# The last batch of a Mamba-and-MoE block in two halves of its tokens

## The chip, the cores and the metric

The kernel runs on one core of one Trainium2 chip. The core has five engines that run side by side and meet through semaphores: PE (TensorE, matmuls and transposes), DVE (VectorE), ACT (ScalarE), POOL (GpSimd) and SP (SyncE, which here issues all DMAs). The metric is the device time of one execution in microseconds, lower is better.

## The reference

The input x is 8 batches of 1024 tokens of 256 channels. One adaptive-norm block is computed, with six modulation vectors per batch from a small matmul:

```
h = layernorm(x) * (1 + ca) + sa
dt, B, C from h (64-wide, 16-wide, 16-wide projections); dt = softplus(...)
state[n] = exp(dt * A[n]) * state[n] + dt * h * B[n]     # 16 states per channel, along the tokens
x = x + ga * (sum over n of state[n] * C[n] + h * D)
h = layernorm(x) * (1 + cb) + sb
x = x + gb * (gated sum of the top 2 of 8 experts, each 256 x 256, with bias)
```

## The kernel before

**Units.** A batch has 256 channels x 16 states = 4096 rows of 1024 tokens. They are worked in 32 units of 128 rows: two halves of the channels (hf), four groups of states (q), four groups of channels (j). For a unit ACT writes the decay into av (`exp`, L544), DVE forms dt·u·B in the PSUM banks BP from B spread over the partitions in the banks BQ and from dd (`mul`, L728), DVE scans along the 1024 tokens into one of 8 buffers h (`scan`, L735), POOL multiplies by C in place (`ch`, L845). After four units PE sums their rows into the PSUM banks Y (`y`, L412) and spreads the next B (`Bs`, L393). After 16 units DVE adds the skip path (`zs`, the skip product, L758), after 32 PE transposes (`z`, L487) and DVE adds the residual (`zX`, L768).

**Before and behind.** Ahead of its units a batch is normalised from XN, transposed, projected, and dt passes softplus in four pieces of 128 channels x 512 tokens (`dl`, five operations on ACT, L578 to L590; `corr` on DVE, L752; `dt`, three on POOL, L854 to L859) in src; SP copies src to dd, four DMAs for each of j and of dt and dt·u (`ddt`, L340; `ddu`, L347). Src holds one hf, so the pieces of the next hf wait for the copies. Behind its units a batch gets statistics (`stat`, L641, L644), `rstd`, `rsb` (L741), normalisation (`xh`, L656), transposes (`xT`), logits (`lg`), their transpose (`lT`), the top 2 (`soft` and `top`, 17 small operations on DVE, L779 to L795), gates through DRAM (`gT`, `gw`, `gr`, `gl`), and the experts: 4 blocks of 256 tokens x 4 pairs of experts. A step takes POOL's product of tokens and gates (`xg`, L877) and 16 matmuls (`f`, L504); a block ends with bias (L509), ACT's read-out (`fE`, L626), transposes (`o`, L476), the add (`oX`, L773) and the store (`out`).

**Order.** Each engine runs its steps in one fixed order. `schedule` gives every step a planned time in units, from the table AT and the batch's start 32·b, sorts them all, and every engine takes its own from the list. So the numbers of AT set the order within an engine and nothing else; the true times come from waits. `before(b)` is placed one batch early, `after(b)` one batch late: the experts of batch 6 stand among the scans of batch 7. The `Bank` class hands out PSUM banks for the small steps; after the last scan the idle banks BP and BQ serve too (TAIL).

## Time and profile before

| | us |
|---|---|
| median of 3 runs | 1278.88 (1278.57 to 1281.31) |
| profiled execution | 1282.32, of which the span is 1280.4 |
| busy: PE, DVE, ACT, POOL | 965.2, 1059.5, 707.2, 1024.5 |
| granted clock of PE, mean | 0.848 of full |

Times of the trace count from the start of the span. A row of a timeline gives start, duration, engine, line, operation, output<-inputs, number of instructions merged, and in brackets the engine's idle time before with what released it.

### The profile page before, as it was taken

The numbers are of one execution on the slowest core, as the hardware profiler recorded it, in microseconds if no ns is written. First come the engines' busy times: TensorE is split into PE (matmuls) and PEld (weight loads), VectorE is DVE, ScalarE is ACT, GpSimd is POOL, SyncE is SP. The second block draws the span as 40 slices with busy tenths as digits, with TensorE's granted clock in tenths as the row PEclk, the third lists the DMA queues.
The fourth block names the chain that finished last, engine by engine and source line by source line (L and its number), as shares of the span: only waits on it lengthen the run. The fifth ranks groups of instructions, "written<-read, shape, count | busy, mean of one in ns | idle before, by whom it ended". The sixth has DMA issues, their size and how long they took to land. (4 is left out here: it accounts for less than half of the span.)

```text
span 1280.4 us, 13483 instructions
## 1 busy us (share of the span) xinstructions
PE 965.2 (75%) x4232; PEld 604.6 (47%) x4232; DVE 1059.5 (83%) x793; ACT 707.2 (55%) x1348; POOL 1024.5 (80%) x512
## 2 busy tenths in 40 slices
PE   5334444588878897788878887789778896789798
PEld 4101112255554564355644655356445564467576
DVE  1399999999999999898999999999989999992100
ACT  5754567555765568465755667456755474333200
POOL 1476777599997999699978999699969999796253
PEclk9665655689888998798988998799879999899799
DMA  4606150636244451537155433436162624412121
GB/s 156 150 15 164 44 121 1 149 105 156 61 111 121 113 143 48 143 100 181 42 118 143 115 105 76 123 108 173 34 157 76 148 75 115 120 47 66 43 75 58
DMA packets 90536, 131.20 MB, mean 102 GB/s; under 512 B 13529, under 2 KB 73505, under 8 KB 90465
## 3 DMA queue, kind: packets, MB, share of 16 engines
q1 hardware_dynamic: 90464, 130.34, 39.2%
q8 instruction: 34, 0.56, 0.2%
q14 instruction: 38, 0.30, 0.1%
HBM read 54.50 MB, written 8.65 MB: 49 GB/s over the span
## 5 line engine op out<-in xcount | busy, mean ns | idle before, releaser
L845 POOL TENSOR_TENSOR h<-h,Cr 128x1024 f32<-128x1024 f32 x256 | 602.0, 2368 | 131.2 <-DVE h L735 131.0
L735 DVE TENSOR_TENSOR_SCAN h<-av,ps 128x1024 f32<-128x1024 f32 x256 | 585.0, 2285 | 18.3 <-DVE ps L728 0.9
L504 PE MATMUL ps<-xg,we 128*128 128x256 f32 x2048 | 514.7, 409 | 29.8 <-POOL xg L877 22.4
L504 PEld LDWEIGHTS ps<-xg,we 128*128 128x128 f32 x2048 | 412.2, 206 | 137.4 <-issue 44.8
L544 ACT ACTIVATE av<-dd,An 128x1024 f32<-128x1024 f32 x256 | 289.9, 1142 | 141.5 <-DVE h L735 134.2
L877 POOL TENSOR_TENSOR xg<-h2T,gbc 128x1024 f32<-128x1024 f32 x128 | 303.5, 2372 | 76.5 <-DMA gbc<-gates 35.3
L728 DVE TENSOR_TENSOR ps<-ps,dd 128x1024 f32<-128x1024 f32 x256 | 315.4, 1232 | 39.9 <-DMA dd<-src 14.1
L412 PE MATMUL ps<-h,gam 128*32 128x512 f32 x1024 | 165.1, 775 | 32.3 <-POOL h L845 17.6
L393 PE MATMUL ps<-S,sel 64*128 64x512 f32 x128 | 56.0, 523 | 65.0 <-DVE ps L728 64.1
L773 DVE TENSOR_TENSOR X<-ps,X 128x512 f32<-128x512 f32 x32 | 22.0, 688 | 99.3 <-PE ps L476 99.1
L598 ACT ACTIVATE Cr<-ps 128x512 f32<-128x512 f32 x64 | 37.9, 593 | 94.5 <-PE ps L453 63.2
L626 ACT ACTIVATE z<-ps,md 128x256 f32<-128x256 f32 x64 | 26.6, 466 | 104.5 <-PE ps L509 104.5
L412 PEld LDWEIGHTS ps<-h,gam 128*32 128x32 f32 x1024 | 31.7, 128 | 109.6 <-issue 84.0
L393 PEld LDWEIGHTS ps<-S,sel 64*128 64x128 f32 x128 | 22.9, 222 | 106.8 <-DVE ps L728 93.8
L854 POOL TENSOR_TENSOR src<-src,sp_t 128x512 f32<-128x512 f32 x32 | 40.7, 1273 | 30.9 <-DVE sp_t L752 30.9
L453 PE MATMUL ps<-S,sel 64*128 64x512 f32 x64 | 34.4, 541 | 40.2 <-ACT Cr L598 26.8
L446 PE MATMUL ps<-rows,wrow 64*128 64x512 f32 x64 | 44.1, 775 | 11.2 <-DVE S L746 8.0
L560 ACT ACTIVATE hT<-ps,md 128x512 f32<-128x512 f32 x32 | 24.5, 770 | 50.7 <-PE ps L432 50.7
L432 PE MATMUL ps<-identf,sp_t 128*128 128x128 f32 x128 | 22.1, 302 | 37.8 <-ACT sp_t L656 31.1
L453 PEld LDWEIGHTS ps<-S,sel 64*128 64x128 f32 x64 | 13.1, 206 | 66.9 <-ACT Cr L598 35.9
L432 PE MATMUL ps<-identf,XN 128*128 128x128 f32 x128 | 26.4, 344 | 22.4 <-DVE S L746 10.1
L859 POOL TENSOR_TENSOR src<-src,hT 128x512 f32<-128x512 f32 x32 | 40.8, 1274 | 2.5
(96 smaller groups left out, 861.8 us busy)
## 6 DMA issues: line engine op xcount, KB each, us to landing
dd<-src SPq DMA_DIRECT2D x512, 128.0 KB, 2.4
gbc<-gates SPq DMA_DIRECT2D x128, 256.0 KB, 3.5
X<-in_x SPq DMA_DIRECT2D x8, 1024.0 KB, 7.3
...
```

Source lines behind the costliest of these rows:

```text
L393: e = pe.matmul(ps[:, BQ + c], sel[R:P, q], S[R:P, b % 2, c * CH:(c + 1) * CH], start=True, stop=True)
L412: e = pe.matmul(ps[32 * j:32 * j + 32, Y + c], gam[:, b % 2, 2 * j + hf], h[:, (4 * g + j) % HS, c * CH:(c + 1) * CH], start=(q == 0), sto ...
L432: e = pe.transpose(bk[:, q * P:(q + 1) * P], (XM[:, q] if w else XN[:, 4 * c + q])[:, hf * P:(hf + 1) * P], identf[:])
L446: e = pe.matmul(bk, wdt[:, hf * P:(hf + 1) * P], dtr[:, c * CH:(c + 1) * CH], start=True, stop=True)
L453: e = pe.matmul(bk, sel[R:P, NQ + q], S[R:P, b % 2, c * CH:(c + 1) * CH], start=True, stop=True)
L504: e = pe.matmul(ps[:, FB, m * 256:(m + 1) * 256], we[:, hf, 2 * ep + e2, m * P:(m + 1) * P], xg[:, i % XG, e2, hf], start=(ep == e2 == m = ...
L544: act.activation(av[:, u % AS], dd[:, j, 0], ACT.Exp, scale=An[:, 0, i:i + 1]).then_inc(s_a, 1)
L728: dve.tensor_tensor(wide(BP), wide(BQ), dd[:, j, 1], ALU.mult).then_inc(s_bm, 1)
L735: dve.tensor_tensor_scan(h[:, u % HS], av[:, u % AS], wide(BP), 0.0, ALU.mult, ALU.add).then_inc(s_scan, 1)
L845: pool.tensor_tensor(h[:, u % HS], h[:, u % HS], Cr[:, q], ALU.mult).then_inc(s_ch, 1)
L859: pool.tensor_tensor(src[:, 1, cs], src[:, 0, cs], hT[:, b % 2, hf, cs], ALU.mult).then_inc(s_dtu, 1)
L877: pool.tensor_tensor(xg[:, i % XG], h2T[:, :, 256 * c:256 * c + 256].unsqueeze(1).to_broadcast([P, 2, 2, 256]), gbc[:, i % GL].unsqueeze(2 ...
```

## The change

Batch 7 (LAST) is worked in 64 half units: 32 over tokens 0 to 511, then 32 over tokens 512 to 1023. `ring` gives each half unit half a buffer of h and av, so there are 16 and 6 places. ACT copies the last column of each state of the first half into `kept` (`keep`), and the scan of the second half starts from it; POOL's product, which overwrites that column, waits for the copy. The banks of b (BP) and B (BQ) alternate, one of each per half unit and per spread. The loads of dd come in four sets of 512 columns (128 DMAs in place of 64), the softplus pieces in the order of the token halves. `zs`, `z`, `zX`, statistics, norm, routing, gates and experts run per half, with planned times of their own (names ending in A and B). The tail banks serve the second half only. In the planner the half units stand 0.55 apart from 3.59 behind the batch's start (`late`), and all other constants of AT have new values as well, so the order of the other batches can shift too. The routing's small tensors, the gates' DMAs and the semaphores are split in the same way (not shown).

```diff
 P, BLK, CH = 128, 8, 512
 NQ, NJ = 4, 4
 UB = 2 * NQ * NJ
-TOTAL = NB * UB
+LAST = NB - 1
+SPLIT = UB * LAST
+TOTAL = SPLIT + 2 * UB
 HS, AS, XG, GL = 8, 3, 2, 2
 EPS = 1e-5
+PACE = 0.55
 BP, BQ, Y, FB, MB = 0, 2, 4, 6, 7
-AT = dict(exp=-1.21, mul=1.08, scan=1.53, ch=6.84, Bs=0.19, y=7.26, stat0=-5.28, stat0s=0.98, rstd0=3.61,
-          rsb0=1.59, xh0=11.0, xh0s=0.0, xT0=14.39, xT0h=1.94, xTs=3.73, rxT0=-0.6, wx=5.18, rwx=-0.33, S=0.3,
-          ldx=33.57, gam=38.49, dl0=20.77, dl1=35.27, dls=3.25, rdl=-0.37, corr=1.62, dt=7.73, C=25.76,
-          CS=2.56, Cc=2.97, rC=-0.32, ddt=36.17, ddts=1.47, ddu=36.38, ddus=1.74, zs=4.09, ldx2=32.55, z=3.84,
-          zX=1.16, zd=1.62, stat1=4.55, stat1s=0.63, rstd1=9.44, rsb1=0.73, xh1=9.97, xh1s=0.0, xh1g=1.34,
-          xT1=11.24, xT1h=0.62, xT1s=1.34, rxT1=-0.73, lg=13.33, rlg=0.11, lT=0.58, rlT=-0.25, soft=2.26,
-          softe=-1.82, top=2.7, gT=1.83, rgT=-0.99, gw=11.19, gr=34.34, xg=22.19, xgs=1.74, gl=-2.54, f=-2.35,
-          fE=0.24, o=2.15, oX=3.12, out=15.62, md1=-34.13, gates=-49.65, ga=-3.38)
+AT = dict(exp=-0.77, mul=1.64, scan=2.24, ch=6.45, Bs=-0.01, y=6.85, stat0=-5.1, stat0s=0.67, rstd0=1.17,
+          rsb0=3.44, xh0=3.56, xh0s=0.32, xT0=13.59, xT0h=2.02, xTs=3.63, rxT0=0.32, wx=4.29, rwx=0.92,
+          S=1.74, ldx=31.71, gam=35.11, dl0=19.88, dl1=34.98, dls=3.7, rdl=0.32, corr=2.11, dt=5.91, C=25.77,
+          CS=3.43, Cc=0.88, rC=0.44, ddt=40.03, ddts=0.91, ddu=41.44, ddus=1.19, zs=4.96, ldx2=33.63, z=4.89,
+          zX=1.12, zd=1.59, stat1=5.89, stat1s=0.4, rstd1=8.89, rsb1=2.35, xh1=9.83, xh1s=0.14, xh1g=1.0,
+          xT1=10.69, xT1h=0.46, xT1s=1.53, rxT1=0.06, lg=12.73, rlg=0.79, lT=0.36, rlT=0.75, soft=3.62,
+          softe=-2.05, top=3.65, gT=1.45, rgT=0.36, gw=14.19, gr=35.16, xg=21.62, xgs=1.76, gl=-5.61, f=-2.15,
+          fE=0.55, o=2.87, oX=4.07, out=18.16, md1=-39.19, gates=-31.77, ga=-39.94, dtL=6.8, dlL0=19.7,
+          dlL1=28.05, dlL2=35.27, dlL3=38.79, defer=-0.1, ddL=-4.28, late=3.59, expL=-3.77, mulL=0.2,
+          scanL=0.49, chL=13.21, BsL=-3.79, yL=10.36, zsL=9.04, keep=1.26, zA=4.6, zB=14.77, zXA=1.0,
+          zXB=19.05, zdA=39.81, zdB=5.99, stat1A=5.26, stat1B=18.11, stat1sA=0.0, stat1sB=0.0, rstd1A=5.8,
+          rstd1B=23.04, rsb1A=1.57, rsb1B=23.92, xh1A=6.93, xh1B=29.62, xh1sA=0.0, xh1sB=1.09, xh1gA=5.05,
+          xh1gB=69.25, xT1A=8.3, xT1B=35.72, xT1hA=1.57, xT1hB=12.51, xT1sA=40.02, xT1sB=22.36, rxT1A=0.0,
+          rxT1B=15.64, lgA=10.75, lgB=60.74, rlgA=0.68, rlgB=7.79, lTA=1.53, lTB=10.67, rlTA=1.33, rlTB=0.15,
+          softA=2.56, softB=43.82, softeA=1.66, softeB=-25.94, topA=3.13, topB=44.68, gTA=7.7, gTB=32.21,
+          rgTA=1.12, rgTB=14.09, gwA=23.22, gwB=64.93, grA=49.62, grB=127.0, xgA=32.58, xgB=140.39,
+          xgsA=12.14, xgsB=14.47, glA=-3.23, glB=14.59, fA=8.35, fB=5.67, fEA=6.12, fEB=12.1, oA=1.07,
+          oB=64.82, oXA=54.06, oXB=87.4, outA=41.88, outB=47.69)
...
-            put(s + AT["corr"], "corr", b, hf, c)
-            put(s + AT["dt"], "dt", b, hf, c)
-        s = t + 16 * hf
+    for i in range(4):
+        hf, c = (i % 2, i // 2) if b == LAST else (i // 2, i % 2)
+        s = t + (AT["dl1" if hf else "dl0"] + AT["dls"] * c if b < LAST else AT[f"dlL{i}"])
+        put(s, "dl", b, hf, c)
+        put(s + AT["rdl"], "read", "dl", b, hf, c)
+        put(s + AT["corr"], "corr", b, hf, c)
+        put(s + AT["dtL" if b == LAST and i > 1 else "dt"], "dt", b, hf, c)
+    for i in range(4 if b == LAST else 2):
+        s = t + (PACE * 16 * i + AT["ddL"] * min(i, 1) if b == LAST else 16 * i)
         for j in range(NJ):
-            put(s + AT["ddt"] + AT["ddts"] * j, "ddt", 2 * b + hf, j)
-            put(s + AT["ddu"] + AT["ddus"] * j, "ddu", 2 * b + hf, j)
+            put(s + AT["ddt"] + AT["ddts"] * j, "ddt", 2 * b + i, j)
+            put(s + AT["ddu"] + AT["ddus"] * j, "ddu", 2 * b + i, j)
     for q in range(NQ):
         for c in range(2):
             s = t + AT["C"] + AT["CS"] * q + AT["Cc"] * c
...
-    for i in range(UB):
-        for n in ("exp", "mul", "scan", "ch"):
-            put(t + i + AT[n], n, UB * b + i)
-    for i in range(2 * NQ):
-        put(t + 4 * i + AT["Bs"], "Bs", 2 * NQ * b + i)
-        put(t + 4 * i + AT["y"], "y", 2 * NQ * b + i)
-    for hf in range(2):
-        put(t + 16 * hf + 16 + AT["zs"], "zs", b, hf)
+    n, pace, own = UB, 1, ""
+    if b == LAST:
+        n, pace, t, own = 2 * UB, PACE, t + AT["late"], "L"
+    for i in range(n):
+        for name in ("exp", "mul", "scan", "ch"):
+            put(t + pace * (i + AT[name + own]), name, UB * b + i)
+        if i < n - UB:
+            put(t + pace * (i + AT["keep"]), "keep", UB * b + i)
+    for i in range(n // 4):
+        put(t + pace * (4 * i + AT["Bs" + own]), "Bs", 2 * NQ * b + i)
+        put(t + pace * (4 * i + AT["y" + own]), "y", 2 * NQ * b + i)
...
-def after(b, t, put):
-    for kp in range(2):
-        s = t + AT["z"] + AT["zd"] * kp
+def after(b, t, put, part=None):
+    halves = range(2) if part is None else (part,)
+    times = AT if part is None else {n: AT[n + "AB"[part]] for n in HALF}
+    blocks = [k for c in halves for k in range(4 * c, 4 * c + 4)]
+    tag = (b,) if part is None else (b, part)
+    for i, kp in enumerate(halves):
+        s = t + times["z"] + times["zd"] * i
         put(s, "z", b, kp)
-        put(s + AT["zX"], "zX", b, kp)
-    for k in range(BLK):
...
         beside(b, UB * b, put)
-        after(b, UB * (b + 1), put)
+        if b < LAST:
+            after(b, UB * (b + 1), put)
+    for part in range(2):
+        after(LAST, SPLIT + AT["late"] + PACE * UB * (part + 1), put, part)
     return [step for _, step in sorted(at, key=lambda p: p[0])]
...
 def unit(u):
-    b, r = divmod(u, UB)
-    return b, r // 16, r // 4 % 4, r % 4
+    b, c = (u // UB, None) if u < SPLIT else (LAST, (u - SPLIT) // UB)
+    return b, u // 16 % 2, u // 4 % 4, u % 4, c
+def piece(b, hf, c):
+    return 4 * b + (2 * c + hf if b == LAST else 2 * hf + c)
+def loads(H):
+    if H < 2 * LAST:
+        return 2 * H + 1, H - 1, 0, 64 * (H + 1)
+    i = H - 2 * LAST
+    return 4 * LAST + i, 2 * LAST - 1 if i < 2 else H - 2, i % 2, 64 * (i // 2 + 1 + (2 * LAST if i % 2 == 0 else 0))
+def ring(u, n):
+    if u < SPLIT:
+        return u % n, slice(0, L), u - n
+    m = SPLIT + (u - SPLIT) // 2
+    return m % n, slice(u % 2 * CH, u % 2 * CH + CH), m - n if m - n < SPLIT else u - 2 * n
+def place(H):
+    return slice(0, L) if H < 2 * LAST else slice(H % 2 * CH, H % 2 * CH + CH)
...
             return self.HEAD
-        if s[:3] == ("xT", 1, NB - 1) or s[0] in ("lg", "lT", "gT", "o") and s[1] == NB - 1:
+        if s[:4] == ("xT", 1, LAST, 1) or s[0] in ("lg", "lT", "gT") and s[1:] == (LAST, 1):
+            return self.TAIL
+        if s[0] == "o" and s[1] == LAST and s[2] >= 2:
             return self.TAIL
...
+                    last, old, r, _ = loads(H)
+                    sp.wait_ge(s_dt, last + 1)
                     if H:
-                        sp.wait_ge(s_a, 16 * (H - 1) + 12 + j + 1)
+                        sp.wait_ge(s_a, 16 * old + 12 + j + 1)
                     for nl in range(4):
-                        sp.dma_start(dd[32 * nl:32 * nl + 32, j, 0], src[32 * j:32 * j + 32, 0]).then_inc(s_ddt[j], 16)
+                        sp.dma_start(dd[32 * nl:32 * nl + 32, j, 0, place(H)], src[32 * j:32 * j + 32, 0, place(H)]
+                                     ).then_inc(s_ddt[r][j], 16)
...
                     for c in range(2):
                         emptied(pe, ("wx", b, c))
-                if g:
-                    pe.wait_ge(s_bm, 4 * g)
-                for c in range(2):
-                    e = pe.matmul(ps[:, BQ + c], sel[R:P, q],
-                                  S[R:P, b % 2, c * CH:(c + 1) * CH], start=True, stop=True)
+                if half is None:
+                    if g:
+                        pe.wait_ge(s_bm, 4 * g)
+                    for c in range(2):
+                        e = pe.matmul(ps[:, BQ + c], sel[R:P, q], S[R:P, b % 2, c * CH:(c + 1) * CH], start=True, stop=True)
...
+                elif q == 0:
+                    pe.wait_ge(s_zr, 2 * b + half)
+                    pe.wait_ge(s_z, 2 * b + 2 * half)
...
+                n, cols, old = ring(u, AS)
+                if old >= 0:
+                    act.wait_ge(s_scan, old + 1)
                 i = 16 * hf + 4 * j + q
-                act.activation(av[:, u % AS], dd[:, j, 0], ACT.Exp, scale=An[:, 0, i:i + 1]).then_inc(s_a, 1)
+                act.activation(av[:, n, cols], dd[:, j, 0, place(u // 16)], ACT.Exp,
+                               scale=An[:, 0, i:i + 1]).then_inc(s_a, 1)
...
-                        for j in range(NJ):
-                            act.wait_ge(s_ddt[j], 64 * (2 * b + hf))
-                            act.wait_ge(s_ddu[j], 64 * (2 * b + hf))
+                    if b == LAST and i % 4 >= 2:
+                        copied(act, 2 * LAST + i % 4 - 2)
+                    elif i % 2 == 0 and i:
+                        copied(act, i // 2 - 1)
...
+                elif s[0] == "keep":
+                    u = s[1]
+                    act.wait_ge(s_scan, u + 1)
+                    n, cols, _ = ring(u, HS)
+                    act.activation(kept[:, u - SPLIT:u - SPLIT + 1], h[:, n, cols.stop - 1:cols.stop], ACT.Copy).then_inc(s_keep, 1)
...
+                if half is None:
+                    dve.tensor_tensor(wide(BP), wide(BQ), dd[:, j, 1], ALU.mult).then_inc(s_bm, 1)
+                else:
+                    dve.tensor_tensor(ps[:, BP + u % 2], ps[:, BQ + u // 4 % 2], dd[:, j, 1, place(u // 16)], ALU.mult).then_inc(s_bm, 1)
...
             def scan(u):
-                if u >= HS:
-                    dve.wait_ge(s_y, (u - HS) // 4 + 1)
+                half = unit(u)[-1]
+                n, cols, old = ring(u, HS)
+                if old >= 0:
+                    dve.wait_ge(s_y, old // 4 + 1)
                 dve.wait_ge(s_bm, u + 1)
                 dve.wait_ge(s_a, u + 1)
-                dve.tensor_tensor_scan(h[:, u % HS], av[:, u % AS], wide(BP), 0.0, ALU.mult, ALU.add).then_inc(s_scan, 1)
+                hu, a = h[:, n, cols], av[:, ring(u, AS)[0], cols]
+                if half is None:
+                    dve.tensor_tensor_scan(hu, a, wide(BP), 0.0, ALU.mult, ALU.add).then_inc(s_scan, 1)
+                else:
+                    i = (u - SPLIT) % UB
+                    start = 0.0
+                    if half:
+                        dve.wait_ge(s_keep, i + 1)
+                        start = kept[:, i:i + 1]
+                    dve.tensor_tensor_scan(hu, a, ps[:, BP + u % 2], start, ALU.mult, ALU.add).then_inc(s_scan, 1)
             def beside_scan(s):
                 if s[0] == "rsb":
...
+                    hf, z, y = i, hT[:, b % 2, i % 2], wide(Y)
+                    if b == LAST:
+                        hf = i % 2
+                        z, y = z[:, i // 2 * CH:(i // 2 + 1) * CH], ps[:, Y + hf]
+                    dve.scalar_tensor_tensor(out=z, in0=z, scalar=Dga[:, hf, b:b + 1], in1=y, op0=ALU.mult,
...
+                n, cols, _ = ring(u, HS)
+                hu, cq = h[:, n, cols], Cr[:, q]
+                if half is not None:
+                    cq = cq[:, half * CH:(half + 1) * CH]
+                    if half == 0:
+                        pool.wait_ge(s_keep, u - SPLIT + 1)
+                pool.tensor_tensor(hu, hu, cq, ALU.mult).then_inc(s_ch, 1)
```

## Rows read from the trace of the kernel before

**Rows 1.** The page's costliest groups: three of them, busy us, mean ns | idle before, releaser.

```profile
L845 POOL TENSOR_TENSOR h<-h,Cr 128x1024 f32<-128x1024 f32 x256 | 602.0, 2368 | 131.2 <-DVE h L735 131.0
L735 DVE TENSOR_TENSOR_SCAN h<-av,ps 128x1024 f32<-128x1024 f32 x256 | 585.0, 2285 | 18.3 <-DVE ps L728 0.9
...
L877 POOL TENSOR_TENSOR xg<-h2T,gbc 128x1024 f32<-128x1024 f32 x128 | 303.5, 2372 | 76.5 <-DMA gbc<-gates 35.3
```

**Rows 2.** Busy time of each engine in four stretches, times from the span's start.

```profile
739.20:876.80 137.60, 112.95 (x518) 71.82 (x517) 131.86 (x96) 84.93 (x162) 123.89 (x60) 0.90 0.43 111
1018.50:1154.30 135.80, 107.43 (x503) 70.87 (x502) 127.27 (x93) 61.28 (x103) 124.74 (x58) 0.90 0.37 95
1154.30:1205.80 51.50, 39.53 (x208) 30.81 (x207) 10.86 (x24) 18.90 (x54) 21.19 (x10) 0.89 0.16 48
1205.80:1280.40 74.60, 67.16 (x288) 55.83 (x288) 2.77 (x4) 3.36 (x8) 35.17 (x15) 0.91 0.23 68
```

**Rows 3.** Timeline of DVE in batch 7: start us, us, line, operation [idle before].

```profile
1019.97 1.23 DVE L728 TENSOR_TENSOR ps<-ps,dd 128x1024 f32<-128x1024 f32 x1 [1.46 <-PE ps L393]
...
1082.42 0.19 DVE L779 TENSOR_REDUCE gs<-ga_t 128x8 f32<-128x64 f32 x1
...
1131.98 1.23 DVE L728 TENSOR_TENSOR ps<-ps,dd 128x1024 f32<-128x1024 f32 x1
1133.30 2.29 DVE L735 TENSOR_TENSOR_SCAN h<-av,ps 128x1024 f32<-128x1024 f32 x1
1135.63 1.23 DVE L728 TENSOR_TENSOR ps<-ps,dd 128x1024 f32<-128x1024 f32 x1
```

**Rows 4.** Four lines by themselves: duration in ns, min/median/max, first and last start.

```profile
L773 DVE TENSOR_TENSOR X<-ps,X x32: 680/691/693, 294.7 to 1277.1; 128x512 f32<-128x512 f32 x32
...
L758 DVE SCALAR_TENSOR_TENSOR hT<-hT,Dga,ps x16: 1270/1276/1281, 129.1 to 1158.8; 128x1024 f32<-128x1024 f32 x16
...
L741 DVE TENSOR_TENSOR rs<-rs x16: 159/1080/3905, 22.5 to 1180.0; 128x8 f32<-128x8 f32 x16
...
L859 POOL TENSOR_TENSOR src<-src,hT x32: 1261/1274/1285, 40.0 to 1063.4; 128x512 f32<-128x512 f32 x32
```

**Rows 5.** Timeline of POOL, batch 7 and the end.

```profile
1021.27 4.67 POOL L845 TENSOR_TENSOR h<-h,Cr 128x1024 f32<-128x1024 f32 x2
...
1092.83 2.36 POOL L845 TENSOR_TENSOR h<-h,Cr 128x1024 f32<-128x1024 f32 x1 [7.31 <-DVE h L735]
1097.67 2.35 POOL L877 TENSOR_TENSOR xg<-h2T,gbc 128x1024 f32<-128x1024 f32 x1 [2.48 <-DMA gbc<-gates]
...
1154.37 2.35 POOL L845 TENSOR_TENSOR h<-h,Cr 128x1024 f32<-128x1024 f32 x1 [0.32 <-DVE h L735]
...
1203.39 4.65 POOL L877 TENSOR_TENSOR xg<-h2T,gbc 128x1024 f32<-128x1024 f32 x2 [18.06 <-DMA gbc<-gates]
```

**Rows 6.** Timeline of PE, the last sums of batch 6.

```profile
1029.86 1.92 PE L412 MATMUL ps<-h,gam 128*32 128x512 f32 x16
```

**Rows 7.** Timeline of ACT, the first exponential behind the third piece's softplus.

```profile
1035.84 1.15 ACT L544 ACTIVATE av<-dd,An 128x1024 f32<-128x1024 f32 x1
```

**Rows 8.** Timeline of SP's queue, four loads of dd.

```profile
1023.50 2.50 SPq L347 DMA_DIRECT2D dd<-src  x4
```

**Rows 9.** Timeline of PE, first steps of the last two expert groups.

```profile
1243.15 3.69 PE L504 MATMUL ps<-xg,we 128*128 128x256 f32 x16 [1.02 <-ACT z L626]
...
1259.72 3.69 PE L504 MATMUL ps<-xg,we 128*128 128x256 f32 x16 [1.02 <-ACT z L626]
```

**Rows 10.** Timeline of ACT, first statistic of two blocks in a row.

```profile
1164.99 0.42 ACT L641 ACTIVATE junk<-X 128x256 bf16<-128x256 f32 x1 [12.82 <-DVE X L768]
...
1166.17 0.42 ACT L641 ACTIVATE junk<-X 128x256 bf16<-128x256 f32 x1
```

**Rows 11.** Timeline of DVE, first and last of 17 routing operations, batch 7.

```profile
1192.71 0.22 DVE L779 TENSOR_REDUCE gs<-ga_t 128x8 f32<-128x64 f32 x1 [11.26 <-ACT ga_t L605]
...
1196.73 0.22 DVE L795 TENSOR_TENSOR ga_t<-ga_t,gs 128x64 f32<-128x64 f32 x1
```

281 lines of the change are left out of this document (165 added, 116 removed).

## The prediction

> **What bounds the kernel now.** I read the groups of instructions first, then the stages, then the order of time around the last batch. The costliest groups are POOL's product by C and DVE's scan, 256 of each; DVE idled 18.3 us before all its scans together [rows 1]. The reader is to see two engines close to full. In a middle period of 137.6 us DVE is busy 131.9 and POOL 123.9 us. In the last batch's scans (1018.5 to 1154.3) both fall a little, and in the last 126 us DVE does nearly nothing: routing until 1205.8, then 74.6 us with PE alone busy [rows 2]. Seven expert steps of batch 6 are still left at 1156.7. So the end is: scans, a chain of norm and routing that nothing covers, then 16 expert steps on PE. The change shortens this tail and lengthens the scans before it.
>
> The profiled execution took 1282.32 us, 1.9 over its span of 1280.4; the median is 1278.88. I make the sum in span and take the difference from the median.
>
> **Price of a half unit.** A unit (product by dt·u, then scan) repeats every 3.65 us, 1.32 to the scan and 2.33 to the next product [rows 3]. A product of 512 columns from PSUM takes 0.691 [rows 4], against 1.23 for 1024 [rows 3]: 0.15 of it is fixed. A scan of 2.29 with the same fixed part gives 1.22 (bounds: 1.14, half, and 1.45). With the gaps seen (0.08 and 0.03) a half unit is 2.03 us, two of them 4.06: +0.41 for each of 32 pairs, 13 us on DVE. POOL: 1.274 for 512 columns [rows 4] against 2.36, a full one repeating every 2.33 (two in 4.67 [rows 5]), so a half one every 1.25: 64 of them 80 us, +5.5.
>
> **The kept states.** 32 copies of one column on ACT lie between its exponentials; for 32 pairs of halves ACT has some 2.0 us per DVE half unit and needs 0.7 (an estimate from the 1.15 of 1024 columns [rows 7]) plus 0.2. I cost them at nothing; where ACT is stuck in another wait, POOL's product waits behind it (rival 2). The scan of a second half reads its start value from SBUF beside av. Such a scalar stands in the skip product, whose 16 runs lie between 1270 and 1281 ns whatever POOL does, while small operations with two SBUF tensors stretch from 159 to 3905 ns [rows 4]. I take +0.04 each, 1.3 us (bounds 0 and, as if stopped, a whole POOL half, 1.25 x 32 = 40).
> The Trainium skill, SBUF — State Buffer, section "SBUF: two separate sides", says that DVE and GpSimd share a port pair as an exclusive lock, which a DVE operation with two SBUF inputs takes against GpSimd. If the kept column counted as such an input, 32 scans would each wait half a POOL product on average, some 20 us; by the skip product's row it doesn't count.
>
> **Up to the routing of batch 6.** Before, DVE goes from 1019.97 to the routing at 1082.42: 62.45 us, 15 units (54.7) and 7.8 of other work [rows 3]. In the new order the routing (16.25 behind the batch's start) stands behind scan 22, since scan u stands at 3.86 + 0.55u. So 23 half units, 46.7, and 7.8: 1074.5 if nothing stalls. I add three stalls. (1) The skip product of batch 6 stands behind 3 half units instead of behind 3 units and a product. It needs POOL's last two products of batch 6, which start at 1021.27 [rows 5], and their sums, which end at 1031.8 [rows 6]; DVE is there at 1026.8: 5 us. (2) ACT's softplus of the second pair of pieces stands behind exponential 3 and lets ACT back at 1035.8 [rows 7]; now it has half units to cover it: 1 us. (3) The fourth piece overwrites source columns that the loads of the new second quarter must have left. Each set of four loads holds SP for 2.5 us [rows 8], eight sets 20 us, behind the first quarter's: until some 1046, while ACT, with the kept copies and exponentials from the 11th on, stands behind it; DVE's correction of that piece stands behind scan 9, due about 1048 with the piece at 1050: 2 us (bounds 0, if an issue of 64 KB is cheaper, and 8). Sum 8: routing at 1082.5, where it was. The first half's dd loads for the second token half have 16 half units of lead and are hidden.
>
> **From the routing to the last product by C.** From routing to the first expert product it is 15.25 us, 1082.42 to 1097.67 [rows 3, 5], the same operations: 1097.8. POOL's order then decides. The product of unit u stands at 10.86 + 0.55u, the expert product k of batch 6 at 21.52 + 1.76k: 20 half products stand before the first expert product, and 14 expert products before the last half product (45.5). Before it was 16 and 9. POOL then has 44 x 1.25 + 14 x 2.33 = 87.6 us without a gap: last product done at 1185.4, against 1156.7 (1154.37 + 2.35 [rows 5]): +28.7. DVE isn't the bound here: from 1089 it has 41 half units (83), two skip products, one residual add, one rsb, the routing of half A (4.3, with POOL in its way 6) and three adds, about 97 us: 1186 if nothing overlaps worse, so the two engines are near each other, and I take POOL's. The double banks of B take away waits such as the 1.46 us before 1019.97 [rows 3]; these are off the bound then.
>
> **The tail.** PE's order is written: sums, expert steps 14 and 15 of batch 6, transposes of half B, then half A's 8 steps with B's transposes, logits and gates between steps 1 and 6, then half B's 8. From the last product on: sums 1.1 and 1.3 for the expert product; two steps of 3.5 with bias and read-out 2.2, out-transposes 0.6 and residual transposes 1.0: 13.2. Half A, two groups at the period of 16.57 (1243.15 to 1259.72 [rows 9]): 33.1. B's pieces on PE between them 2.6. Stalls: B's statistics are 4 blocks of 1.18 [rows 10], with rstd, rsb and four normalisations 8.5 us behind the residual add, beside two steps of 3.5: 2.7. Its 17 small operations take 4.2 (1192.71 to 1196.95 [rows 11]) beside steps 4 and 5: 0. Step 7's gates stand on SP behind an output of half A whose add stands behind B's routing: 1.5. First B step at +53. From a group's start with two groups left it is 37.25 (1243.15 to 1280.4 [rows 9]). Tail 90.3, against 123.7: -33.4. The B gates leave SP at about +42 and need 5.7 (POOL from 1203.39 [rows 5]): hidden under steps 6 and 7, with 3 us to spare.
>
> Sum: +28.7 - 33.4 = -4.7: span 1275.7, median 1274.2. The other seven batches keep the order of DVE's operations but for shifts under a unit (rsb and the XN normalisation come earlier), at 0; bounds -1 and +1 us a batch.
>
> **Rivals.**
> 1. The head stalls don't come (POOL and PE finish batch 6 earlier under half units, or SP issues 64 KB faster): routing at 1074.5, C's last at 1177.4, median 1266. For it: SP's durations in rows 8 say nothing of 64 KB. Against: the sums end at 1031.8 whatever DVE does.
> 2. Slower: ACT stands in the fourth piece's wait for the second quarter's loads, and the kept copies from the 6th or so on stand behind it, so POOL stands too, though its columns are scanned. 64 more loads cost 38 us of SP in the batch. If they land 12 us later than the 1046 above, routing comes at 1094.5 and the median is 1286. It decides from 7 us on (then the gain of 4.7 turns into a loss above 0.2%). Before, ACT waited there only for loads of the half before.
> 3. The kept column takes the port (above): 20 us on DVE's second half, which has little slack, +15: 1289. The rows speak against it.
> 4. No change: half A's steps fill PE anyway, and what the halves save is what they cost: within 2.6 us. It is the forecast with 3 us more, in the tail or on POOL.
>
> **How the numbers follow.** The measurement tells 0.2%, 2.6 us, from no change. Forecast 50% (own range 1267 to 1280; of it 36 faster, 12 same, 2 slower); rival 1 22%; rival 2 20%; rival 3 3%; the reordered other batches by themselves 5% (2 faster, 1 same, 2 slower; rival 4 is in the forecast's range). Faster 60%, same 13%, slower 27%. Range 1258 to 1290: rival 1 with the batches' gain below, rivals 2 and 3 above.
>
> **What would show it.** Scans of 1.22 and products by C of 1.27; no idle POOL between its first batch-6 expert product and its last product by C; routing of batch 6 within 3 us of 1082; DVE idle some 5 us before batch 6's last skip product; last product by C at 1180 to 1190; 90 us from there to the end; PE without a gap over 3 us after the first A step. It is wrong if DVE or ACT bounds the second half, if the second half's scans are longer than the first's, or if A's expert steps run among the scans.

## The result and the profile after

The changed kernel takes 1301.41 us, the median of 4 runs (1300.04 to 1302.13), beside 1279.85 for the kernel before on the same chip: ratio 1.0167, 95% interval 1.0149 to 1.0184. Forecast were 1274.2, in a range of 1258 to 1290. It is slower by 21.6 us, and the time lies outside the range. The profiled execution took 1302.13 us with a span of 1300.3, 19.9 more than the span before.

The groups of the page, as in [rows 1], show the operations at the prices that were worked out: the units of the first seven batches are unchanged, and the half units of the last take 1.22 and 1.28 us to scan and 1.25 for the product by C (80.0 us for 64). These are the groups with shapes kept apart:

```profile
L1009 POOL TENSOR_TENSOR h<-h,Cr 128x1024 f32<-128x1024 f32 x224 | 527.4, 2371 | 128.7 <-DVE h L882 127.3 <-ACT Cr L718 1.3
...
L1009 POOL TENSOR_TENSOR h<-h,Cr 128x512 f32<-128x512 f32 x64 | 80.0, 1288 | 12.5 <-DVE h L889 7.1 <-ACT kept L798 5.4
...
L889 DVE TENSOR_TENSOR_SCAN h<-av,kept,ps 128x512 f32<-128x512 f32 x32 | 41.0, 1280 | 2.7
...
L889 DVE TENSOR_TENSOR_SCAN h<-av,ps 128x512 f32<-128x512 f32 x32 | 39.0, 1219 | 3.2 <-DVE ps L871 0.4 <-ACT av L655 0.4
```

So the loss isn't in the price of a half unit. The next view is the busy time in four stretches: a middle batch (from its first scan to the next batch's, the same events as the first row of [rows 2]); from the last scan of batch 6 to 1156.7, inside POOL's mix of products by C and expert products; from there to the end of the last product by C; and the tail. The columns are the stretch, its length, busy PE, PEld, DVE, ACT and POOL with counts, granted clock, DMA share, GB/s:

```profile
749.30:888.20 138.90, 113.41 (x517) 70.31 (x516) 131.53 (x98) 87.07 (x168) 124.40 (x61) 0.90 0.44 113
1031.30:1156.70 125.40, 102.65 (x454) 67.54 (x458) 110.91 (x130) 71.88 (x179) 103.67 (x69) 0.85 0.40 107
1156.70:1201.30 44.60, 35.29 (x173) 23.87 (x166) 41.45 (x50) 9.63 (x19) 37.50 (x27) 0.89 0.19 42
1201.30:1300.30 99.00, 85.41 (x373) 69.00 (x371) 12.93 (x25) 13.84 (x38) 42.28 (x19) 0.91 0.20 59
```

The last scan of batch 6 ends at 1031.3, where before it ended at 1018.5 [rows 2]. The reader is to see that 12.8 of the 19.9 us are there before the first half unit has run, in batches that the halving doesn't touch. The whole decomposition, cut at the same events before and after, in us of span:

| stretch | before | after | change | forecast |
|---|---|---|---|---|
| start to last scan of batch 6 | 1018.5 | 1031.3 | +12.8 | 0 |
| to the first expert product of batch 6 on POOL | 79.2 | 73.5 | -5.7 | 0 |
| to the end of the last product by C | 59.0 | 96.5 | +37.5 | +28.7 |
| to the end of the span | 123.7 | 99.0 | -24.7 | -33.4 |

**Where the first 12.8 us go.** The small product `rsb` (eight columns, two SBUF inputs; L741 before, L896 now) has a line of its own in [rows 4]: 159/1080/3905 ns before. The same view of it after, with the scans beside it:

```profile
L896 DVE TENSOR_TENSOR rs<-rs x17: 141/1904/6792, 22.8 to 1222.7; 128x8 f32<-128x8 f32 x15, 128x4 f32<-128x4 f32 x2
...
L889 DVE TENSOR_TENSOR_SCAN h<-av,kept,ps x32: 1280/1280/1283, 1118.9 to 1198.7; 128x512 f32<-128x512 f32 x32
...
L916 DVE SCALAR_TENSOR_TENSOR hT<-hT,Dga,ps x18: 722/1266/1273, 129.5 to 1204.5; 128x1024 f32<-128x1024 f32 x14, 128x512 f32<-128x512 f32 x4
```

The median is 1.9 us and the longest 6.8, for an operation that takes 0.14 when alone. The scans with a kept start, and the skip product, don't stretch at all. What a long one waits for shows when the timelines of DVE and POOL are laid side by side. DVE in batch 2:

```profile
323.77 2.28 DVE L882 TENSOR_TENSOR_SCAN h<-av,ps 128x1024 f32<-128x1024 f32 x1
325.96 6.49 DVE L896 TENSOR_TENSOR rs<-rs 128x8 f32<-128x8 f32 x1
332.38 1.22 DVE L869 TENSOR_TENSOR ps<-ps,dd 128x1024 f32<-128x1024 f32 x1
```

And POOL at the same time, where a row without brackets follows the one before it without a gap:

```profile
323.06 2.45 POOL L1009 TENSOR_TENSOR h<-h,Cr 128x1024 f32<-128x1024 f32 x1
325.37 2.47 POOL L1042 TENSOR_TENSOR xg<-h2T,gbc 128x1024 f32<-128x1024 f32 x1
327.68 4.75 POOL L1009 TENSOR_TENSOR h<-h,Cr 128x1024 f32<-128x1024 f32 x2
335.45 1.26 POOL L1019 TENSOR_TENSOR src<-src,sp_t 128x512 f32<-128x512 f32 x1 [3.02 <-DVE sp_t L907]
```

`rsb` starts at 325.96 while POOL works and ends at 332.45; POOL's last product ends at 332.43. It has sat out not one operation of POOL but the rest of three, until POOL ran out of work. Then POOL waits in its turn, 3.02 us, for what DVE should have made. At 898.23 it is the same: 6.79 us, to 905.02, and POOL's run ends at 904.99 (900.29 + 4.70).

Not every wait is of this kind. In batch 4 `rsb` gets in behind one product by C, and POOL goes on without a gap:

```profile
648.01 1.90 DVE L896 TENSOR_TENSOR rs<-rs 128x8 f32<-128x8 f32 x1
```

```profile
647.55 2.35 POOL L1009 TENSOR_TENSOR h<-h,Cr 128x1024 f32<-128x1024 f32 x1
649.86 2.35 POOL L1042 TENSOR_TENSOR xg<-h2T,gbc 128x1024 f32<-128x1024 f32 x1
```

Of the 17 `rsb` of this kernel 13 are stretched. Each ends within 0.03 us of the end of an operation of POOL: seven at the first one's end with POOL going on, two where POOL's only operation left ends, four behind two or three operations, at the end of POOL's run. What decides between the two kinds no run shows; the four take 22.6 of the 39.6 us.

The Trainium skill, SBUF — State Buffer, section "SBUF: two separate sides", says that the pair of ports is held "for the whole instruction" by whoever starts first, while the other blocks. The trace agrees that the small product blocks, and nine of the 13 waits fit one instruction of the other. The other four don't: 6.49 us is longer than any POOL instruction in these rows (2.47 at most). The measurement decides.

**The last batch.** A wait of the long kind stands here in the routing of the first half. DVE, with the routing of the first half between the scans:

```profile
1171.65 0.70 DVE L871 TENSOR_TENSOR ps<-ps,dd 128x512 f32<-128x512 f32 x1
1172.26 0.17 DVE L937 TENSOR_REDUCE gs<-ga_t 128x4 f32<-128x32 f32 x1
1172.47 7.23 DVE L938 TENSOR_TENSOR ga_t<-ga_t,gs 128x32 f32<-128x32 f32 x1
1179.73 0.18 DVE L939 TENSOR_SCALAR ga_t<-ga_t 128x32 f32<-128x32 f32 x1
1179.95 1.28 DVE L889 TENSOR_TENSOR_SCAN h<-av,kept,ps 128x512 f32<-128x512 f32 x1
```

POOL works until 1179.65 and is then short of scans:

```profile
1178.34 1.31 POOL L1009 TENSOR_TENSOR h<-h,Cr 128x512 f32<-128x512 f32 x1
1181.31 1.27 POOL L1009 TENSOR_TENSOR h<-h,Cr 128x512 f32<-128x512 f32 x1 [1.66 <-DVE h L889]
1186.91 1.27 POOL L1009 TENSOR_TENSOR h<-h,Cr 128x512 f32<-128x512 f32 x1 [4.33 <-DVE h L889]
...
1193.75 1.27 POOL L1009 TENSOR_TENSOR h<-h,Cr 128x512 f32<-128x512 f32 x1 [0.83 <-DVE h L889]
```

**The tail.** SP's queue has two stores standing before gates that the experts wait for:

```profile
1215.17 0.38 SPq L470 DMA_DIRECT2D out<-X  x1
1215.64 0.91 SPq L465 DMA_DIRECT2D gbc<-gates  x1
...
1245.68 0.38 SPq L470 DMA_DIRECT2D out<-X  x1
1246.15 1.30 SPq L465 DMA_DIRECT2D gbc<-gates  x1
```

POOL, which multiplies tokens by these gates, idles beside them (the first gap is put down to PE, the last to come of two; the gates had only just been asked for at 1215.64):

```profile
1220.26 4.66 POOL L1042 TENSOR_TENSOR xg<-h2T,gbc 128x1024 f32<-128x1024 f32 x2 [9.70 <-PE ps L610]
...
1250.57 2.34 POOL L1042 TENSOR_TENSOR xg<-h2T,gbc 128x1024 f32<-128x1024 f32 x1 [5.69 <-DMA gbc<-gates]
```

### The profile page after: what moved, and what is told of

It reads as the page before. It is cut to its first block and busy times, and to the rows that moved or that the text cites. A ratio compares the mean times of both kernels' runs of the same rounds, so it can differ in the third digit from the quotient of the medians.

```text
span 1300.3 us, 13889 instructions
## 1 busy us (share of the span) xinstructions
PE 983.2 (76%) x4235; PEld 612.4 (47%) x4235; DVE 1090.1 (84%) x877; ACT 724.1 (56%) x1418; POOL 1029.8 (79%) x544
## 5 line engine op out<-in xcount | busy, mean ns | idle before, releaser
L1009 POOL TENSOR_TENSOR h<-h,Cr 128x1024 f32<-128x1024 f32 (+1 forms) x288 | 607.4, 2131 | 141.2 <-DVE h L882 127.3
L882 DVE TENSOR_TENSOR_SCAN h<-av,ps 128x1024 f32<-128x1024 f32 x224 | 511.7, 2284 | 14.9 <-DVE ps L869 0.9
L655 ACT ACTIVATE av<-dd,An 128x1024 f32<-128x1024 f32 (+1 forms) x288 | 299.4, 1047 | 149.6 <-DVE h L882 114.1
L869 DVE TENSOR_TENSOR ps<-ps,dd 128x1024 f32<-128x1024 f32 x224 | 276.0, 1232 | 40.8 <-DMA dd<-src 15.5
L517 PE MATMUL ps<-h,gam 128*32 128x512 f32 x1024 | 157.7, 738 | 19.1 <-POOL h L1009 15.9
L491 PEld LDWEIGHTS ps<-S,sel 64*128 64x128 f32 x112 | 21.0, 232 | 114.3 <-DVE ps L869 101.2
L558 PE MATMUL ps<-S,sel 64*128 64x512 f32 x64 | 36.3, 570 | 30.7 <-ACT Cr L718 23.9
L546 PE MATMUL ps<-hT,wx 128*128 128x512 f32 x64 | 43.6, 818 | 18.2 <-DVE sp_t L907 9.2
L698 ACT ACTIVATE sp_t<-ps,bd 128x512 f32<-128x512 f32 x32 | 21.8, 682 | 55.8 <-PE ps L551 55.7
L781 ACT ACTIVATE sp_t<-X,rs 128x256 f32<-128x256 f32 x64 | 34.0, 588 | 26.0 <-DVE rs L896 26.0
L871 DVE TENSOR_TENSOR ps<-ps,dd 128x512 f32<-128x512 f32 x64 | 44.7, 698 | 3.8
```

The lines of the kernel that those rows point to most:

```text
L491: e = pe.matmul(ps[:, BQ + c], sel[R:P, q], S[R:P, b % 2, c * CH:(c + 1) * CH], start=True, stop=True)
L517: e = pe.matmul(ps[32 * j:32 * j + 32, Y + (c if half is None else hf)], gam[:, b % 2, 2 * j + hf], h[:, n, cols.start + c * CH:cols.start ...
L546: e = pe.matmul(bk, wx[:, k], hT[:, b % 2, k, c * CH:(c + 1) * CH], start=(k == 0), stop=(k == 1))
L655: act.activation(av[:, n, cols], dd[:, j, 0, place(u // 16)], ACT.Exp, scale=An[:, 0, i:i + 1]).then_inc(s_a, 1)
L869: dve.tensor_tensor(wide(BP), wide(BQ), dd[:, j, 1], ALU.mult).then_inc(s_bm, 1)
L871: dve.tensor_tensor(ps[:, BP + u % 2], ps[:, BQ + u // 4 % 2], dd[:, j, 1, place(u // 16)], ALU.mult).then_inc(s_bm, 1)
```

## The experiments

The theory after the result has three parts. **Order:** the new constants of AT, not the halves, cost the first 13 us, because `rsb` of the first norm stands at a place where POOL's runs are long, and DVE waits for them. **Stores:** two stores in SP's order hold gates back, 9 us. **Routing:** the first half's routing waits on the path, up to 7 us. The rival to each is that the halves cost by themselves: kept states, more loads, more waits.

Each kernel has its ratio to the kernel before on the same chip, with a 95% interval. Where a kernel is compared with another of the table, it is by these ratios, or by the medians where that is said.

**1. The new order without the halves.** The kernel before with the shared constants of the new AT; all batches whole.

```diff
-AT = dict(exp=-1.21, mul=1.08, scan=1.53, ch=6.84, ... rstd0=3.61, rsb0=1.59, xh0=11.0, ...
+AT = dict(exp=-0.77, mul=1.64, scan=2.24, ch=6.45, ... rstd0=1.17, rsb0=3.44, xh0=3.56, ...
```

> The kernel before, whole batches, with the new values of the planner's constants (order changes, nothing is halved). Theory A, the new order costs the first seven batches 11 to 13 us whatever the last batch does: about 1291. Rival, those 11 us come with the halving (its queue entries, its loads): 1280. With A, the first norm's rsb (the product of negative mean and rstd on DVE) is stretched in this kernel as in the changed one, 6 us in several batches against 3.9 before.

Measured: 1292.23 us, ratio 1.0102 (1.0082 to 1.0122). The first scan of the last batch starts at 1035.6, against 1021.3 before and 1032.2 in the changed kernel. So the order alone costs 13 us; the halves with all that belongs to them cost the rest, 8 to 9. The 16 `rsb` take 39.5 us here.

**2. The old order under the halves.** The changed kernel; the other batches get the old constants, shifted by one amount for each engine (ACT +0.44, DVE +0.56, POOL -0.39, PE -0.41, SP +3.0) so that they meet the last batch. The first scan constants as an example:

```diff
-AT = dict(exp=-0.77, mul=1.64, scan=2.24, ch=6.45, ...
+AT = dict(exp=-0.77, mul=1.64, scan=2.09, ch=6.45, ...
```

> The changed kernel, last batch in halves, with the old order for all other batches (old constants, each engine's shifted by one amount so that they fit the last batch's). Theory A: 1301 less 11 to 13, about 1289; what is left over 1280 is the halving's own, 9 us. Rival, the order of the first seven batches is innocent: 1300.

Measured: 1311.3 us, ratio 1.0253 (1.023 to 1.0275). A miss. `rsb` does get shorter (1200 ns in the mean of 15), but other waits come in: DVE stands 30.7 us for PE's B, and POOL 53.7 us for gates. The last batch's first scan is at 1044.5; the period before it is 154.3 us. Probably the shifted engines no longer fit one another; that wasn't tested, and this kernel tells nothing of the halves.

**3 and 4. `rsb` off DVE, in both kernels.** The eight columns are multiplied on ACT, one small operation each with the factor as its scale, right behind the rsqrt.

```diff
+                    act.wait_ge(s_rd[w], nth(s[1:]))
+                    for k in range(k0, k1):
+                        e = act.activation(rs[:, w, 5, k:k + 1], rs[:, w, 0, k:k + 1], ACT.Identity, scale=rs[:, w, 4, k:k + 1])
+                    e.then_inc(s_rs[w], 1)
...
-                    dve.tensor_tensor(rs[:, w, 5, k0:k1], rs[:, w, 0, k0:k1], rs[:, w, 4, k0:k1], ALU.mult).then_inc(s_rs[w], 1)
```

> The changed kernel with rsb taken from DVE: 8 (or 4) small operations on ACT behind rstd form the same product. Theory B: DVE's operation with two SBUF inputs waits until POOL's run of operations ends, and these waits (rsb busy 39.6 us in 17 operations, 37 of them waiting) stand on the bound: 1301 less 15 to 30, so 1271 to 1286. Rival, POOL is the bound wherever DVE waits for it, so that nothing is won: 1298 to 1302.

> The kernel before with rsb on ACT in the same way. Theory B: its 16 rsb are busy 25.3 us, 22.7 of them waiting: 1280 less 10 to 20, 1260 to 1270. Rival, POOL is the bound while DVE waits: 1278 to 1281.

Measured: with halves 1266.8 us, ratio 0.99 (0.9884 to 0.9915); the kernel before with the same edit 1266.9, ratio 0.9899 (0.9874 to 0.9923). The edit is worth 34.6 us by the medians in the changed kernel, more than the 15 to 30 expected, and 13 in the one before; the two are then equal. So of the 25.3 us that `rsb` took before, at the prices of [rows 4], about half was on the path all along. The edit also spares ACT the way over DVE and back (ACT waited 43.3 us for `rs` in the changed kernel); what of the gain is that and what is DVE's time isn't separated. ACT pays 25.6 us for it (128 operations, beside its waits), and both kernels are faster all the same:

```profile
L792 ACT ACTIVATE rs<-rs 128x1 f32<-128x1 f32 x128 | 25.6, 281 | 0.6
```

**5. The new order, whole batches, `rsb` on ACT.** Edits 1 and 3 together.

> Whole batches in the new order, with rsb on ACT. Theory B says that the new order is slow only through the longer waits of rsb; the split kernel with rsb on ACT reaches its last batch's first scan at 997.8, and from there the kernel before needs 259: 1257 span, about 1259 to 1261, and the halving then costs 6 to 8 us. Rival, the halves gain in this order and rsb hid it: 1267 or more.

Measured: 1261.49 us, ratio 0.9842 (0.9808 to 0.9877). Without the wait of `rsb` the new order isn't worse than the old but 5 us (medians) to 7 us (ratios) better (0.9842 beside 0.9899, whose intervals just meet). The last batch's first scan starts at 999.6 against 1004.8. So the new order has no net loss but that of `rsb`. The halves in this order and with `rsb` on ACT (kernel 3, 0.99) cost 5 to 7 us; kernel 10 shows where they go.

**6. The first norm alone put back.** The changed kernel; six constants have their old values, so `rsb` of the first norm stands behind the multiply of a batch's unit 3 instead of behind the scan of unit 2 (units counted from 0; in the kernel before it stood behind the multiply of unit 4).

```diff
-AT = dict(... stat0=-5.1, stat0s=0.67, rstd0=1.17, rsb0=3.44, xh0=3.56, xh0s=0.32, ...
+AT = dict(... stat0=-5.28, stat0s=0.98, rstd0=3.61, rsb0=1.59, xh0=11.0, xh0s=0.0, ...
```

> The kernel after, with six constants of the first norm (sums, rsqrt, the four copies after it, the products with x) put back to those of the kernel before. The copies then stand behind the third multiply and the product with x of batches 0 to 6 and before the third scan, not behind the second scan, and the rsqrt on ACT stands late again. Everything else stays in the new order, the halves too. Theory port wait by place: the new place of the first norm's four copies is what makes them wait on GpSimd's long runs (39.6 us of VectorE against 25.3 before), and most of the +12.8 us until the last scan of batch 6. Then the last batch's first scan comes at 1022 to 1026 us instead of 1032.2, the four copies hold VectorE 25 to 30 us in all, and the time is 1289 to 1294. Rival other constants: the +12.8 comes from the rest of the new order (scans, correction, logits, gathers); the copies are late in any place, hold VectorE for 36 us or more, and the time is 1298 to 1303.

What the expectation calls the four copies is `rsb`, one product of eight columns.

Measured: 1291.19 us (10 runs, 1285.24 to 1297.45), ratio 1.0072 (1.0048 to 1.0096). The first scan of the last batch starts at 1019.1 in the profile, 13.1 earlier than in the changed kernel, earlier than the 1022 to 1026 expected and no later than before. The time is in the range expected. The six constants move ACT's steps of that norm as well, but ACT's new order did no harm in kernel 5, so it is the place of `rsb` that the loss hangs on. The operation itself is still long: its 17 runs take 32.6 us, above the 25 to 30 expected and below the 39.6 of the changed kernel. It is 7.0 us shorter and the kernel 10 (medians) to 12 us (ratios) faster; where the rest comes from wasn't traced. In batch 2 of this kernel:

```profile
329.38 4.75 DVE L895 TENSOR_TENSOR rs<-rs 128x8 f32<-128x8 f32 x1
334.05 2.27 DVE L881 TENSOR_TENSOR_SCAN h<-av,ps 128x1024 f32<-128x1024 f32 x1
```

Its runs spread over 12 us (those of the other kernels over 2 to 12), and the profiled execution, 1285.49, is at the low end; so the 13.1 are more than the 12 us by which the ratios differ.

**7. The two stores later.** The changed kernel; the store of batch 6's last block is planned 8 units later, those of the first half 3 later (41.88 to 45.0).

```diff
-        put(s + times["out"], "out", b, c)
+        put(s + times["out"] + (8 if tag == (LAST - 1,) and c == 3 else 0), "out", b, c)
```

> The changed kernel with two stores moved behind gate loads in SP's order: the store of batch 6's last block behind half A's second gate load, that of half A's first block behind half A's last. Theory D: these stores wait for adds and hold the gate loads, 3 us at half A's second step and 3.6 us at its eighth: 1301 less 4 to 7. Rival, the gates of half B set the end anyway: less than 1.

Measured: 1291.76 us, ratio 1.0081 (1.0053 to 1.0108). That is 9.6 us by the medians and 11 by the ratios, more than the 4 to 7 expected. The last product by C ends at 1201.84, the span at 1291.6: a tail of 89.7 us instead of 99.0. The gates behind the moved store are asked for by 1206.9, where it was 1215.64, and POOL's waits at these steps are for PE (for gates of the second half it still stands 3.08 and 5.03 us later on):

```profile
1208.74 2.35 POOL L1041 TENSOR_TENSOR xg<-h2T,gbc 128x1024 f32<-128x1024 f32 x1 [2.26 <-PE ps L609]
1213.22 2.35 POOL L1041 TENSOR_TENSOR xg<-h2T,gbc 128x1024 f32<-128x1024 f32 x1 [2.13 <-PE ps L617]
1220.88 2.36 POOL L1041 TENSOR_TENSOR xg<-h2T,gbc 128x1024 f32<-128x1024 f32 x1 [5.30 <-PE ps L609]
```

**8. The first half's routing left out.** The changed kernel without 15 of the 17 operations of that routing on DVE; the gates of the first half are then not the ones of the reference.

> The changed kernel without 15 of the 17 routing operations of half A on DVE (its top 2 isn't formed, the gates of half A are stale). Theory C: the first of them with two SBUF inputs stands 7.2 us until POOL's run ends and POOL then starves 6 us: last product by C 8 to 11 us earlier (7.2 and 3.2 of operations), the whole 1301 less 6 to 10. Rival, POOL's queue is the bound in that stretch and only DVE moves: less than 2.

Measured: 1294.79 us, ratio 1.0087 (1.0045 to 1.0128), 6.6 us less than the changed kernel by the medians and 10 by the ratios, whose intervals don't overlap. POOL has no wait for a scan left in its mixed stretch, which is 90.8 us instead of 96.5. The last product by C ends 3.8 us earlier (1197.5), where 8 to 11 were expected; the profiled execution is the slowest of the five.

**9. The same routing behind the last scan.** Nothing is left out; three constants put its 17 operations behind the scans.

```diff
-AT = dict(... softA=2.56, ... topA=3.13, ... gTA=7.7, ...
+AT = dict(... softA=6.75, ... topA=6.8, ... gTA=10.5, ...
```

> The kernel after, with three constants of the first half's routing in the last batch made larger, so that its 17 VectorE operations stand behind the last scan of the batch instead of between its last two channel blocks. Theory port wait on the path: the 7.23 us operation at 1172.47 goes out of the scans, the last scan of the batch ends about 6 us earlier, GpSimd doesn't starve for 1.66 and 4.33 us, and its last product ends near 1195 instead of 1201.3; the first half's experts start later, but they stand behind the gathers on GpSimd, which come after the products anyway, so the time is 1294 to 1298. Rival cover gone: the first half's routing behind the scans delays its gathers by the 10 us that the scans gain, the gathers of both halves come together at the end, and the time is 1301 to 1308.

Measured: 1300.76 us, ratio 1.0146 (1.0113 to 1.0179), not told apart from the changed kernel. POOL's stretch from the first expert product to the last product by C is 90.3 us (1109.38 to 1199.66) and has no wait for a scan, 6.2 less than after; but its last product was expected near 1195, the last batch's first scan comes 3.1 us later in this profile, and the tail grows to 101.5. The time lies between the two forecasts (1294 to 1298 and 1301 to 1308). Moved behind the scans, the routing meets the expert products on POOL, and six of its operations are stretched, four of them here:

```profile
1194.61 1.41 DVE L937 TENSOR_TENSOR ga_t<-ga_t,gs 128x32 f32<-128x32 f32 x1
1196.06 1.18 DVE L938 TENSOR_SCALAR ga_t<-ga_t 128x32 f32<-128x32 f32 x1
...
1199.74 2.29 DVE L944 SCALAR_TENSOR_TENSOR ga_t<-ga_t 128x32 f32<-128x32 f32 x1
...
1202.28 2.04 DVE L946 TENSOR_TENSOR ga_t<-ga_t,gs 128x32 f32<-128x32 f32 x1
```

The 17 now end at 1206.1, 11.7 us behind the first, where 4.2 are work [rows 11]. One of the six is the compare (L938), which has a single tensor as its input. What 8 shows as the price can't be had by moving the routing there.

**10. `rsb` on ACT and the stores later, with halves.** Edits 3 and 7; run twice, the second time beside kernels 11 to 13.

> The changed kernel with rsb on ACT and the two stores moved. If both add up: 1266.8 less 4 to 7, so 1260 to 1263. If the stores matter only where rsb waits: 1266.

> The changed kernel with rsb on ACT and the two stores moved, as run before, here as the base of the pauses: 1259, 0.984 of the kernel before.

Measured: 1259.19 us, ratio 0.9842 (0.9799 to 0.9885), and 1259.46, ratio 0.9827 (0.9796 to 0.9857). Whole batches in the same order had 0.9842 (kernel 5). The halves gain nothing that can be told from zero.

**11 and 12. A pause for POOL.** If DVE waits until POOL runs out of work, POOL can be made to stop where DVE needs the port. Kernel 11 is kernel 10 with two waits on POOL, ahead of a product and of an expert product in the first half's routing (first and last part of the cut); kernel 12 adds one for the routing of each of batches 0 to 5, ahead of product 13 of the next batch (middle part).

```diff
+                if u == SPLIT + 53:
+                    pool.wait_ge(s_lg, NB)
+                if u < SPLIT and u > UB and u % UB == 13:
+                    pool.wait_ge(s_g, u // UB)
...
+                    if (b, c, ep) == (LAST - 1, 2, 3):
+                        pool.wait_ge(s_g, NB)
```

> The same with two waits added on POOL beside half A's routing: its product 53 of the last batch waits for the first three routing operations, the expert product behind product 54 for the last one. Theory C: DVE's operation with two SBUF inputs waits for the end of POOL's run, 7.3 us there; if POOL stands still it starts at once, DVE is 5 us earlier at the last scans and POOL starves less: 4 to 6 us less than the base, by adding waits. Rival, the lock goes to DVE within one POOL operation and the 7.3 us have another cause: the waits only cost, 1 to 4 us more.

> The same, and in batches 1 to 6 POOL's product 13 waits until the routing of the batch before is through. There DVE stands 4.5 us a batch behind POOL's last two products (2.24 and 2.30 us for operations of 0.2) and POOL starves afterwards. Theory C: 2 to 4 us a batch, so 12 to 24 less than with half A's pause alone. Rival, POOL's products 13 and 14 come too late for the sums and the scans behind: nothing or a loss of up to 4 us a batch.

Measured: 1256.13 us, ratio 0.9797 (0.9764 to 0.9829), where the interval overlaps that of kernel 10, so that the 3.3 us by the medians (4 to 6 expected) aren't told from zero; and 1248.48 us, ratio 0.9736 (0.9709 to 0.9763), which doesn't overlap. Kernel 12 is 7.7 us under kernel 11 by the medians, in the direction of the theory but less than its 12 to 24.

**13. The pauses with whole batches.** Kernel 5 with the wait ahead of product 13, here for the routing of batch 6 too.

> Whole batches in the new order, rsb on ACT, and the pause at product 13 in batches 1 to 7. 1261 less 2 to 4 us a batch: 1233 to 1249 by theory C, 1261 to 1285 by the rival. Against the kernel in halves with all pauses it shows what the halving brings once its two stores and the waits at the port are out of the way: 5 us in favour of the halves by theory C, since the sum of the prediction was -4.7.

Measured: 1246.97 us, ratio 0.9723 (0.9695 to 0.9752). It beats both kernels, by 2.8% the one before. The time is in the range expected; the 5 us in favour of the halves didn't come (kernel 12 has 1248.48). One routing of this kernel, with POOL stopped:

```profile
372.78 0.19 DVE L779 TENSOR_REDUCE gs<-ga_t 128x8 f32<-128x64 f32 x1
373.00 0.23 DVE L780 TENSOR_TENSOR ga_t<-ga_t,gs 128x64 f32<-128x64 f32 x1
373.26 0.20 DVE L781 TENSOR_SCALAR ga_t<-ga_t 128x64 f32<-128x64 f32 x1
...
376.77 0.23 DVE L795 TENSOR_TENSOR ga_t<-ga_t,gs 128x64 f32<-128x64 f32 x1
```

And POOL around it:

```profile
363.72 6.98 POOL L847 TENSOR_TENSOR h<-h,Cr 128x1024 f32<-128x1024 f32 x3
377.17 4.70 POOL L847 TENSOR_TENSOR h<-h,Cr 128x1024 f32<-128x1024 f32 x2 [6.47 <-DVE ga_t L795]
```

The two-input operation of the routing (L780) takes 0.23 us here, and 2.36 in the middle of the nine in the changed kernel (L938). POOL stands 6.47 us here, and by the medians the kernel is 14.5 us faster than kernel 5. Without the pause POOL ran one product more at this routing (number 13 of the batch) and then stood 7.57 us for a scan, so that product 14 starts at 383.26, where with the pause it starts at 379.50. This is kernel 5:

```profile
373.33 2.36 POOL L845 TENSOR_TENSOR h<-h,Cr 128x1024 f32<-128x1024 f32 x1 [0.18 <-DVE h L739]
383.26 2.35 POOL L845 TENSOR_TENSOR h<-h,Cr 128x1024 f32<-128x1024 f32 x1 [7.57 <-DVE h L739]
```

**What a last batch costs in each.** From the first scan of the last batch to the end of the span, in us:

| | stretch | halves |
|---|---|---|
| before | 259.1 | no |
| 1, new order | 258.3 | no |
| after | 268.1 | yes |
| 3, `rsb` on ACT | 265.3 | yes |
| 4, `rsb` on ACT, old order | 257.9 | no |
| 7, stores later | 258.8 | yes |
| 5, `rsb` on ACT | 260.4 | no |
| 10, `rsb` on ACT, stores later | 259.0 and 260.9 | yes |
| 11, first pauses | 254.6 | yes |
| 12, pauses | 254.1 | yes |
| 13, pauses | 254.1 | no |

## Why the prediction was wrong

**"The other seven batches keep the order of DVE's operations but for shifts under a unit (rsb and the XN normalisation come earlier), at 0; bounds -1 and +1 us a batch."** This is the step that failed first: +12.8 us, where it had 0 (kernels 1 and 6). The shift was seen, and named, and priced by its distance, which was read too short as well: `rsb` of the first norm moved from behind the multiply of unit 4 to behind the scan of unit 2, a unit and a half. The price is set by what POOL does at the new place. The bound of 1 us a batch would have allowed 7; batch 2 alone took 6.1 more (147.3 beside 141.2 before, by the first scans of batches 2 and 3). [Rows 4] had the evidence: the prediction read 3905 ns off that row to argue for the kept start value and didn't ask what the same row says of `rsb` itself.

**What bounds the kernel.** One reading is wrong: in the last batch's scans only DVE falls (131.9 to 127.3 us); POOL, said to fall too, goes from 123.9 to 124.7 in a shorter stretch [rows 2]. Nothing in the sum rests on it.

**Half units, kept column.** Right. Product 0.70, scan 1.22, POOL 1.25 apart; the kept start costs 0.06 instead of 0.04, and the 32 durations lie between 1280 and 1283 ns, whatever POOL does. Rival 3 is refuted for the scans. Its mechanism was real and struck elsewhere: on `rsb` and on the routing's first operation with two inputs in SBUF, which they both have. The kept copies take 0.19 us each, and the forecast costed them at nothing.

**Up to the routing of batch 6.** The sum counted from the batch's start gave 62.5 us (1019.97 to 1082.5); it took 60.3 (1031.43 to 1091.73). Of the three head stalls the first has the forecast size by luck: DVE idled 5.2 us, where 5 were forecast, but before the add of an expert block, which waited for PE's transposes behind 16 matmuls that took 5.4 us together, and not before the skip product, which then didn't wait. ACT's wait in the fourth piece was 3.2, against 2. Rival 2 happened in small and decided nothing. A kept copy did stop POOL once, for 5.4 us, behind another wait: ACT stood for batch 6's routing on DVE (3.5 us) and for PE (2.9), and the copy of half unit 19, behind both, came 14.4 us after its scan. It cost nothing, since POOL's next expert product had its gates only at 1104.8. From the routing to the first expert product it was 13.1 instead of 15.25. Together the stretch is 5.7 us shorter than before, of which most isn't the halves' doing: with pauses it is 72.8 us in halves and 72.3 in whole batches (kernels 12 and 13).

**"POOL then has 44 x 1.25 + 14 x 2.33 = 87.6 us without a gap."** The work is right, the "without a gap" isn't: 96.5 us. POOL stood 7.1 us for scans (1.66, 4.33, 0.83, 0.28) and 2.7 for PE. The prediction had the first half's routing at 6 us on DVE "with POOL in its way" and DVE and POOL near each other, and took POOL's number; the routing took 7.2 us in one operation, and then DVE was the bound. By kernel 8 it is worth 6.6 to 10 us (by medians, and by ratios 1.0167 and 1.0087, whose intervals don't overlap); kernel 9 shows that it isn't free behind the scans either. Without any wait for a scan the stretch is still 90.3 to 90.8 us (kernels 8 and 9), the rest being waits for PE that the sum had at nothing.

**The tail, -33.4.** The form was right and one queue was left out. With the two stores out of the way the tail is 89.7, against 90.3 forecast (kernel 7). The prediction did ask what stands before step 7's gates on SP (1.5 us), and not what stands before the first ones: a store waits for its add, the add for the block's last step and transposes, and behind it wait gates that are long ready. This is 9.3 us by the profiles and 9.6 by the medians.

**The net of the halving.** Forecast -4.7. With the stores moved it is -0.3 by the stretch above (259.1 to 258.8; counted from the last scan of batch 6, whose half unit then follows 1.9 us sooner, -2.2), and it stays at nothing with `rsb` on ACT (0.9842 both) and with pauses (0.9736 and 0.9723, intervals overlapping). The tail shortened by 34.0 us is real. It is paid back by 37.5 us of POOL, of which the forecast had 28.7. Kernels 12 and 13 differ by the halves and by where the last pauses stand: from the last scan of batch 6 on, the halves add 0.5 us in the head and 32.7 in POOL's stretch (92.9 beside 60.2) and take 34.1 from the tail, -0.9 in all. So the step that was mis-sized in the halving itself is POOL's stretch: its work is 87 us as forecast, and 2.9 us for PE and 3.4 in the two pauses of the first half's routing stand beside it in kernel 12.
